# One ScalarE instruction writes the first f16 part of a tile to both of its places; VectorE copies only the second part

## The chip, the core and the metric

The kernel runs on one core of a Trainium2 chip. Its engines are TensorE (PE in the profile; PEld is its weight load), VectorE (DVE), ScalarE (ACT), GpSimd (POOL) and SyncE (SP). The metric is the device time of one execution in microseconds, as the median of several runs; lower is better.

## The reference

Eight sequences of 256 tokens with 512 features go through two layers. Layer 0 is a causal self-attention whose keys and values are both a context tensor (16 heads of 32), followed by a mixture of 32 experts (top 8). Layer 1 is a cross-attention with projected and RMS-normalised queries and keys, an output projection, and a ternary linear layer. Cut to what matters here:

```python
x = x + tanh(g_xattn[0]) * causal_attention(layernorm(x), ctx, ctx)          # layer 0: scores = q k^T per head
x = x + tanh(g_ffn[0])   * top8_of_32_experts(layernorm(x), gate_w, w_gate, w_up, w_down)
q = rms_norm(layernorm(x) @ w_q.T + b_q, g_q); k = rms_norm(ctx @ w_k_img.T + b_k_img, g_k_img)
x = x + tanh(g_xattn[1]) * (softmax(q k^T * s) v @ w_o.T + b_o)              # layer 1
x = x + tanh(g_ffn[1])   * (layernorm(x) @ ternary(weight).T + bias)
```

## The kernel before, in words

The program has three stages, one after the other: layer 0's attention, the experts, layer 1's attention.

**The f16 parts.** TensorE works on f16 operands, but f32 accuracy is wanted. So a f32 tile is split into a first part `hi = f16(x * scale)` and a second part `lo = f16(x * scale - hi)`. For the scores each head of 32 features gets four slots of 32 in the tile `parts[:, j, head, 0:4, :]`, so that the 128 rows of one matmul sum all products of parts. A query tile (`j < QT`, that is j = 0, 1) has the order hi, hi, lo, lo; a key tile (j = 2, 3) has hi, lo, hi, lo. `act_hi` on ScalarE writes the hi part to slot 0 (L349), `dve_lo` on VectorE computes the lo part (L355), waits for it, and then duplicates both parts into the two slots that are left with one copy of 1024 elements (L361). TensorE then transposes the finished tile in 16 small transposes (`pe_stack`, L372), and VectorE or ScalarE copies the result out of PSUM (`dve_stack`, L379, or `act_stack`, L318) to where the score matmuls read it.

**The attention loop.** Both layers run a loop of 8 batches (sequences) by 16 steps; each step is two heads of one query tile. A step has the score matmuls (L240, with a mask matmul L243 in layer 0), the row maximum on VectorE (L325) and its bias (L327), the exponential on ScalarE (L293), a transpose on TensorE (L278), a copy of it on ScalarE (L305), and the product with the values (L258). Tables written by hand (`PREP0`, `POST0`, `PREP1`, `POST1`) put the side work of the next batch (prep) and of the batch before (post) into given steps of each engine. Every engine runs its instructions in program order and meets the others by semaphores. In layer 0 the hi parts of the two context tiles are the piece "c" in step 3 on ScalarE (behind the piece "y0", L681, of the post work) and step 4 on VectorE; those of the two query tiles are the piece "q" in step 6, behind "S1" (L318). In layer 1 the four tiles are the pieces k0 to k3, one at a time, in steps 7, 8, 10 and 11 on ScalarE. Each layer splits 4 tiles for each of 8 batches, 64 tiles in all; the first 4 of each layer are split ahead of its loop.

**The experts.** 160 blocks of 128 tokens pass through a software pipeline. In step t TensorE transposes the input of block t+1 (L1293), multiplies block t by the gate and up weights (`gate_up`, L1305, 12 matmuls), transposes the hidden tile of block t-2 (L1316) and multiplies block t-3 by the down weights (L1329). `gate_up(t)` waits for the weights and for `h_ready` of block t-2, which VectorE's last instruction on that block sets (L1420). When a new expert begins, VectorE also splits its weights, in an early part at the end of one step (L1433 and L1436) and a late part at the start of the next (L1436). At the start of each step TensorE and VectorE load a number from a table in SBUF (`t_pe`, L1335, and `t_dve`, L1449) that says which expert comes and what to split. SyncE does the same with its own table (`t_x`, L1157), and its load already has bounds in the source (`min_val`, `max_val`).

Of the kernel before, what the change touches and what calls it, by code (L numbers as in the profile page):

```python
# [15 lines left out]
ACT = mybir.ActivationFunctionType  # L16
# [5 lines left out]
QT = S // P  # L22
HC = H // P
NH, D = 16, 32
# [65 lines left out]
def rep(ap, n, at):  # L90

    dims = [list(d) for d in ap.ap]
    dims.insert(at, [0, n])
    return bass.AP(ap.tensor, ap.offset, dims)
# [96 lines left out]
class Attention:  # L191
# [154 lines left out]

    def act_hi(self, act, b, i, src, scale):
        act.wait_ge(self.stack_ps, 8 * b.n + 2 * i + 2)
        self.nc.scalar.activation(self.part(ORDER[i], 0), src.rearrange("p (h d) -> p h d", d=D), ACT.Copy, scale=scale)\  # L349
          .then_inc(self.hi_ready, 1)  # L350

    def dve_lo(self, dve, b, i, src, scale, chain):
        j = ORDER[i]
        dve.wait_ge(self.hi_ready, 4 * b.n + i + 1)
        chain.link(self.nc.vector.scalar_tensor_tensor(self.part(j, 1), src.rearrange("p (h d) -> p h d", d=D), scale,  # L355
                                                       self.part(j, 0), ALU.mult, ALU.subtract))
        if j < QT:
            dup, of = self.parts[:, j, :, 1:4:2, :], self.parts[:, j, :, 0:4:2, :]
        else:
            dup, of = self.parts[:, j, :, 2:4, :], self.parts[:, j, :, 0:2, :]  # L360
        self.nc.vector.tensor_copy(dup, of).then_inc(self.parts_ready, 1)  # L361

    def pe_stack(self, pe, b, k):

# [746 lines left out]
def experts(nc, shared, plan, proj, w_experts, mats, ternary, ctx, vecs):  # L1111

    es = ExitStack()
    with es:
# [166 lines left out]
        @block.tensor  # L1281
        def _(pe):
            id32, id16 = shared.id32, shared.id16

            pe.sem_inc(y_ps, 1)

            def turn(t):
                pe.wait_ge(x_in[t.place], 16 * t.oct + 16)
                if t.at(-2).exists():
                    pe.wait_ge(x_ready, t.n - 1)  # L1290
                rows, o = xg[:, t.place, 0:H].bitcast(F16), bX[t.place % 2][:, :].bitcast(F16)
                for c in range(2 * HC):
                    last = nc.tensor.transpose(o[:, c * P : (c + 1) * P], rows[:, c * P : (c + 1) * P], id16[:])  # L1293
                last.then_inc(x_ps, 1)

            def gate_up(t, e):
                w = e & (NW - 1)
                pe.wait_ge(x_ready, t.n + 1)
                pe.wait_ge(weights_ready, e + 1)
                if t.at(-2).exists():  # L1300
                    pe.wait_ge(h_ready, t.n - 1)
                passes = [(0, wh), (0, wl), (H, wh)]
                for c in range(HC):
                    for k, (xo, wp) in enumerate(passes):
                        last = nc.tensor.matmul(bGU[t.place % 2][:, 0:GU], xT[:, t.place % 2, xo + c * P : xo + (c + 1) * P],  # L1305
                                                wp[:, bass.ds(w, 1), c * GU : (c + 1) * GU].rearrange("p a w -> p (a w)"),
                                                start=c == 0 and k == 0, stop=c == HC - 1 and k == 2)
                last.then_inc(gu_ps, 1)

            def turn_h(t):  # L1310
                pe.wait_ge(h_ready, t.n + 1)
                if t.at(-2).exists():
                    pe.wait_ge(ht_ready, t.n - 1)
                o = bHT[t.place % 2][:, :].bitcast(F16)
                for c in range(3):
                    last = nc.tensor.transpose(o[:, c * P : (c + 1) * P], hp[:, t.place % 2, c * P : (c + 1) * P], id16[:])  # L1316
                last.then_inc(ht_ps, 1)

            def down(t, e):
                w = e & (NW - 1)  # L1320
                pe.wait_ge(ht_ready, t.n + 1)
                if t.at(-2).exists():
                    pe.wait_ge(y_ready, t.n - 1)
                hi, lo, rest = (hT[:, t.place % 2, c * P : (c + 1) * P] for c in range(3))
                full, part = HC * GU, HC * GU + H
                products = [(hi, wh, full), (hi, wl, full), (lo, wh, full), (rest, wh, part),
                            (rest, wl, part)]
                for k, (h, wp, at) in enumerate(products):
                    last = nc.tensor.matmul(bY[t.place % 2][:, :], h,  # L1329
                                            wp[:, bass.ds(w, 1), at : at + H].rearrange("p a w -> p (a w)"),  # L1330
                                            start=k == 0, stop=k == len(products) - 1)
                last.then_inc(y_ps, 1)

            def step(t):
                code = pe.value_load(t_pe[0:1, t.column()])  # L1335
                e, before = code & (E - 1), code >> 5
                if t.at(1).exists():
                    turn(t.at(1))
                gate_up(t, e)
                if t.at(-2).exists():  # L1340
                    turn_h(t.at(-2))
                if t.at(-3).exists():
                    down(t.at(-3), before)
            turn(Tile(0, 0, 0))
            over_tiles(pe, step)
            last = Tile(MT - 1, (MT - 1) % 8, (MT - 1) // 8)
            turn_h(last.at(-1))
            turn_h(last)
            for t in (last.at(-2), last.at(-1), last):
                down(t, pe.value_load(t_e[0:1, t.column()]))  # L1350
# [51 lines left out]
        @block.vector  # L1402
        def _(dve):
            v = nc.vector

            def hidden(t):
                dve.wait_ge(silu, t.n + 1)
                if t.exists() and t.at(-1).exists():
                    dve.wait_ge(h_ready, t.n)
                v.scalar_tensor_tensor(hv[:, :], bGU[t.place % 2][:, FI:GU], SC_H / (SC_N * SC_W), sg[:, t.place % 2, :],  # L1410
                                       ALU.mult, ALU.mult).then_inc(h_made, 1)
                dve.wait_ge(h_made, t.n + 1)
                if t.at(-2).exists():
                    dve.wait_ge(ht_ps, t.n - 1)
                p, rest = hp[:, t.place % 2, :], FI - P
                v.tensor_copy(p[:, 0:P], hv[:, 0:P]).then_inc(h_hi, 1)
                v.tensor_copy(p[:, 2 * P : 2 * P + rest], hv[:, P:FI]).then_inc(h_hi, 1)
                dve.wait_ge(h_hi, 2 * t.n + 2)
                v.tensor_tensor(p[:, P : 2 * P], hv[:, 0:P], p[:, 0:P], ALU.subtract)
                v.tensor_tensor(p[:, 2 * P + rest :], hv[:, P:FI], p[:, 2 * P : 2 * P + rest], ALU.subtract).then_inc(h_ready, 1)  # L1420


            LATE = 3 * WEXP // 10

            def split(e, freed, early, late):

                w = e & (NW - 1)
                pick = lambda m, a, b: m[:, bass.ds(e & (NR - 1) if m is raw else w, 1), a:b].rearrange("p a w -> p (a w)")
                if early:
                    if freed is not None:  # L1430
                        dve.wait_ge(y_ps, freed + 1)
                    dve.wait_ge(raw_ready, e + 1)
                    v.tensor_scalar(pick(wh, 0, WEXP), pick(raw, 0, WEXP), SC_W, None, ALU.mult).then_inc(w_hi, 1)  # L1433
                dve.wait_ge(w_hi, e + 1)
                for a, b in ((0, LATE),) * early + ((LATE, WEXP),) * late:
                    last = v.scalar_tensor_tensor(pick(wl, a, b), pick(raw, a, b), SC_W, pick(wh, a, b), ALU.mult, ALU.subtract)  # L1436
                if late:
                    last.then_inc(weights_ready, 1)

            for t in range(3):  # L1440
                e = dve.value_load(t_e[0:1, t : t + 1])
                if t == 0:
                    split(e, None, True, True)
                else:
                    with dve.If(dve.value_load(t_new[0:1, t : t + 1]) > 0):
                        split(e, None, True, t == 1)

            def step(t):
                code = dve.value_load(t_dve[0:1, t.column()])  # L1449
                with dve.If((code & 1) > 0):  # L1450
                    split((code >> 2) & (E - 1), None, False, True)
                hidden(t)
                with dve.If((code & 2) > 0):
                    split((code >> 7) & (E - 1), code >> 12, True, False)

            over_tiles(dve, step, turn=4)


# [503 lines left out]
```

## Time and profile before

| | |
|---|---|
| median of 3 runs | 1558.1 us (1552.81, 1558.10, 1558.12) |
| span of the profiled execution, first to last instruction | 1525.3 us |
| median less span | 32.8 us |
| layer 0's attention | about 0 to 265 us of the span |
| experts | about 345 to 960 us |
| layer 1's attention | about 1012 to 1525 us |
| busy share of the span: PE, DVE, ACT, POOL | 86%, 64%, 60%, 34% |

The profiled execution has no time of its own outside the trace, so its span stands beside the median of the runs: the span leaves out what lies before the first and behind the last instruction of the program. A busy share is a mean over three stages with different limits. In the rows further down, a timeline row has its start and its length in us, the engine, the line, the operation, output<-input and the count, and in square brackets how long the engine was idle ahead of it and which instruction ended that.

### The profile page before, as it was taken

How to read it: one execution, taken by the hardware profiler on the slowest of the kernel's cores; microseconds unless marked ns; L12 is line 12 of the kernel's file. 1: busy time of each engine (PE TensorE's matmuls, PEld its weight loads, DVE VectorE, ACT ScalarE, POOL GpSimd, SP SyncE). 2: the span in 40 equal slices, each digit the busy share in tenths (PEclk: the TensorE clock that was granted, in tenths of full speed). 3: DMA queues.
4: the chain of work that ended last, by engine and by line, in shares of the span. 5: the costliest groups of instructions: out<-in, count | busy, mean ns of one | idle time of the engine just before them, and what ended most of it. 6: DMA issues, size and time to landing. Idle time of an engine off the chain costs nothing.

```text
span 1525.3 us, 37150 instructions
## 1 busy us (share of the span) xinstructions
PE 1309.4 (86%) x10733; PEld 834.6 (55%) x10734; DVE 972.8 (64%) x2387; ACT 920.1 (60%) x2261; POOL 520.1 (34%) x531
## 2 busy tenths in 40 slices
PE   5888888837999999999999999477989889898984
PEld 3656655524556666665666666144556555555552
DVE  5888888755456665655655633255787777776853
ACT  4777777724556666666666666244766667667661
POOL 1044444455333433332000001665554444541000
PEclk9988888968999999999999999688999999999997
DMA  2044344458888767767676545775654555642000
GB/s 72 29 173 180 146 146 151 156 213 304 269 285 282 256 219 261 238 217 244 218 242 222 181 149 154 126 111 83 98 99 65 104 82 84 100 65 52 15 1 28
DMA packets 96131, 233.39 MB, mean 153 GB/s; under 512 B 11808, under 2 KB 11808, under 8 KB 91424
## 3 DMA queue, kind: packets, MB, share of 16 engines
q0 software_dynamic: 33712, 113.79, 29.8%
q1 hardware_dynamic: 62320, 118.34, 23.3%
q8 instruction: 55, 0.90, 0.3%
q14 instruction: 44, 0.36, 0.1%
HBM read 140.84 MB, written 91.24 MB: 152 GB/s over the span
## 4 chain that ended last, share of the span: by engine, by line
PE 45%; DMA 9%; DVE 9%; issue 8%; ACT 3%; POOL 3%; SPq 1%; DVEq 0%; ACTq 0%; POOLq 0%
PE bank L1305 18%; PE bank L1329 10%; PE bank L1542 6%; DMA xs<-y_tiles,slot_ix 5%; PE bank L1293 4%; PE bank L258 2%; PE bank L1316 1%; PE bank L278 1%; DMA xg<-x_slots 1%; DVE l_nmax L325 1%; PE bank L1548 1%; POOL xs L430 1%; DMA x_slots<-blank 1%; DVE l_stack L379 1%; PE bank L240 1%
## 5 line engine op out<-in xcount | busy, mean ns | idle before, releaser
L1305 PE MATMUL bank<-wh,xT 128*128 x1280 | 343.3, 330 | 4.7 <-DVE hp L1420 4.4
L430 POOL DMA_INDIRECT xs<-y_tiles,slot_ix x120 | 194.6, 1622 | 234.2 <-DMA y_tiles<-ysb 99.1
L293 ACT ACTIVATE l_probs<-bank,l_bias 128x256 f32<-128x256 f32 (+1 forms) x512 | 224.4, 449 | 64.4 <-DVE l_bias L327 64.0
L1305 PE MATMUL bank<-wl,xT 128*128 x640 | 211.4, 330 | 0.0
L325 DVE TENSOR_REDUCE l_nmax<-bank 128x2 f32<-128x512 f32 (+1 forms) x256 | 158.1, 617 | 70.8 <-PE bank L240 41.3
L1410 DVE SCALAR_TENSOR_TENSOR hv<-bank,sg 128x192 f32<-128x192 f32 x160 | 56.9, 356 | 227.5 <-ACT sg L1364 203.5
L1379 ACT ACTIVATE ysb<-bank,xg 128x512 f32<-128x512 f32 x160 | 109.9, 687 | 119.1 <-PE bank L1329 119.1
L305 ACT ACTIVATE l_probsT<-bank 128x512 f32<-128x512 f32 (+1 forms) x256 | 140.0, 547 | 65.6 <-PE bank L278 65.2
L1358 ACT ACTIVATE xT<-bank 128x1024 f16<-128x1024 f16 x160 | 162.5, 1016 | 15.0 <-PE bank L1293 14.8
L1305 PEld LDWEIGHTS bank<-wh,xT 128*128 128x128 f16 x1280 | 126.5, 99 | 81.3 <-issue 11.1
L1329 PE MATMUL bank<-wh,hT 128*128 x480 | 156.1, 380 | 0.9 <-issue 0.9
L240 PE MATMUL bank<-l_stack 128*128 128x256 f16 (+1 forms) x512 | 105.7, 275 | 59.1 <-ACT l_probs L293 49.3
L278 PE MATMUL bank<-id,l_probs 128*128 128x128 f32 x896 | 149.7, 286 | 2.1 <-ACT l_probsT L305 0.5
L699 POOL DMA_INDIRECT x_slots<-room,slot_ix x112 | 113.4, 1013 | 108.3 <-issue 47.0
L1542 PE MATMUL bank<-w_hi,halfT 128*128 128x512 f16 x384 | 125.9, 390 | 18.9 <-DVE accb L1659 17.1
L1200 POOL DMA_DIRECT2D raw<-in_experts_dram x30 | 16.8, 560 | 334.1 <-DVE wl L1436 333.8
L1364 ACT ACTIVATE sg<-bank 128x192 f32<-128x192 f32 x160 | 52.8, 330 | 113.8 <-PE bank L1305 113.8
L1329 PE MATMUL bank<-wl,hT 128*128 x320 | 121.4, 379 | 0.0
L1293 PEld LDWEIGHTS bank<-id,xg 128*128 128x128 f16 x1280 | 84.9, 99 | 58.7 <-DMA xg<-x_slots 22.6
L1293 PE MATMUL bank<-id,xg 128*128 128x128 f16 x1280 | 98.9, 221 | 19.1 <-DMA xg<-x_slots 18.9
L278 PEld LDWEIGHTS bank<-id,l_probs 128*128 128x128 f32 x896 | 102.6, 147 | 11.7 <-ACT l_probsT L305 7.4
L1436 DVE SCALAR_TENSOR_TENSOR wl<-raw,wh x64 | 95.4, 1491 | 20.0 <-issue 15.9
(246 smaller groups left out, 2538.1 us busy)
## 6 DMA issues: line engine op xcount, KB each, us to landing
xg<-x_slots SPq DMA_DIRECT2D x160, 272.0 KB, 2.8
y_tiles<-ysb SPq DMA_DIRECT2D x160, 256.0 KB, 2.5
raw<-in_experts_dram POOLq DMA_DIRECT2D x30, 1280.0 KB, 7.1
x_slots<-blank SPq DMA_DIRECT2D x33, 272.0 KB, 3.6
xs<-in_x_dram SPq DMA_DIRECT2D x8, 512.0 KB, 4.4
cbuf<-in_ctx_dram SPq DMA_DIRECT2D x8, 512.0 KB, 5.8
stage<-in_mats_dram POOLq DMA_DIRECT2D x4, 1024.0 KB, 7.8
room<-in_ctx_dram SPq DMA_DIRECT2D x8, 512.0 KB, 4.6
```

Of the source, the lines that this page charges most:

```text
L240: last = self.nc.tensor.matmul(o, self.stack[:, b.par, 0, h, qt * P : (qt + 1) * P], self.stack[:, b.par, 1, h, 0:nk], start=True, stop=no ...
L278: last = self.nc.tensor.transpose(self.pT[s % len(self.pT)][:, (2 * kt + u) * P : (2 * kt + u + 1) * P], self.probs[:, s % 2, u, kt * P : ...
L293: last = self.nc.scalar.activation(self.probs[:, s % 2, u, 0:nk], self.pS[s % 2][:, u * S : u * S + nk], ACT.Exp, bias=self.bias[:, s % 4, ...
L305: self.nc.scalar.activation(self.probsT[:, s % 2, 0:w], self.pT[s % len(self.pT)][:, 0:w], ACT.Copy).then_inc(self.probsT_made, 1)
L325: self.nc.vector.tensor_reduce(self.nmax[:, s % 4, :], v, AX, ALU.max).then_inc(self.max_made, 1)
L430: return nc.gpsimd.indirect_dma_start(to, None, self.y_tiles[0 : (MT + 1 - k) * P, :], ix, compute_op=ALU.add)
L699: nc.gpsimd.indirect_dma_start(shared.x_slots, bass.IndirectOffsetOnAxis(ap=slot_ix[:, QT * b.n + t, k % TOPK : k % TOPK + 1], axis=0), xe ...
L1293: last = nc.tensor.transpose(o[:, c * P : (c + 1) * P], rows[:, c * P : (c + 1) * P], id16[:])
L1305: last = nc.tensor.matmul(bGU[t.place % 2][:, 0:GU], xT[:, t.place % 2, xo + c * P : xo + (c + 1) * P], wp[:, bass.ds(w, 1), c * GU : (c + ...
L1329: last = nc.tensor.matmul(bY[t.place % 2][:, :], h, wp[:, bass.ds(w, 1), at : at + H].rearrange("p a w -> p (a w)"), start=k == 0, stop=k ...
L1358: nc.scalar.activation(xT[:, t.place % 2, :], bX[t.place % 2][:, :].bitcast(F16), ACT.Copy).then_inc(x_ready, 1)
L1542: last = nc.tensor.matmul(o, xT[:, xo + c * P : xo + (c + 1) * P], w[:, c * H : (c + 1) * H], start=n == 0, stop=n == len(todo) - 1)
```

## The change

Three edits.

```diff
     def act_hi(self, act, b, i, src, scale):
         act.wait_ge(self.stack_ps, 8 * b.n + 2 * i + 2)
-        self.nc.scalar.activation(self.part(ORDER[i], 0), src.rearrange("p (h d) -> p h d", d=D), ACT.Copy, scale=scale)\
+        j = ORDER[i]
+        twice = self.parts[:, j, :, 0:2, :] if j < QT else self.parts[:, j, :, 0:3:2, :]
+        self.nc.scalar.activation(twice, rep(src.rearrange("p (h d) -> p h d", d=D), 2, 2), ACT.Copy, scale=scale)\
           .then_inc(self.hi_ready, 1)

     def dve_lo(self, dve, b, i, src, scale, chain):
...
-        if j < QT:
-            dup, of = self.parts[:, j, :, 1:4:2, :], self.parts[:, j, :, 0:4:2, :]
-        else:
-            dup, of = self.parts[:, j, :, 2:4, :], self.parts[:, j, :, 0:2, :]
-        self.nc.vector.tensor_copy(dup, of).then_inc(self.parts_ready, 1)
+        self.nc.vector.tensor_copy(self.parts[:, j, :, 3, :], self.part(j, 1)).then_inc(self.parts_ready, 1)
```

The source of the ScalarE instruction is read twice (a repeated dimension of stride 0), 1024 elements instead of 512, and goes to both hi slots. The copy on VectorE moves 512 elements instead of 1024. No instruction is added or taken away here, and the waits are the same.

```diff
             def step(t):
-                code = pe.value_load(t_pe[0:1, t.column()])
+                code = pe.value_load(t_pe[0:1, t.column()], min_val=0, max_val=E * E)
...
             for t in range(3):
-                e = dve.value_load(t_e[0:1, t : t + 1])
+                e = dve.value_load(t_e[0:1, t : t + 1], min_val=0, max_val=E - 1)
...
             def step(t):
-                code = dve.value_load(t_dve[0:1, t.column()])
+                code = dve.value_load(t_dve[0:1, t.column()], min_val=0, max_val=2**24)
```

These give three table loads of the experts' stage bounds, and a load with bounds is followed by instructions that test them. They stand in the program as two more instructions behind each load (shown as ISA x2). On VectorE, at the late part of a weight split, a step begins like this before (`raw` is an expert's loaded weights, `wl` their second f16 part, ISA a register instruction):

```order
L1453 UNCONDITIONAL_BRANCH
L1449 ISA
L1449 TENSOR_LOAD t_dve
L1450 REGISTER_ALU
L1450 COMPARE_AND_BRANCH
L1434 REGISTER_ALU x3
L1436 REGISTER_ALU
L1436 ISA
L1436 REGISTER_ALU
L1436 ISA
L1436 SCALAR_TENSOR_TENSOR wl<-raw,wh 128x1792
```

and like this in the changed program, whose line numbers are two lower there:

```order
L1451 UNCONDITIONAL_BRANCH
L1447 ISA
L1447 TENSOR_LOAD t_dve
L1447 ISA x2
L1448 REGISTER_ALU
L1448 COMPARE_AND_BRANCH
L1432 REGISTER_ALU x3
L1434 REGISTER_ALU
L1434 ISA
L1434 REGISTER_ALU
L1434 ISA
L1434 SCALAR_TENSOR_TENSOR wl<-raw,wh 128x1792
```

Nothing else moved; the two instructions stand between the load and the branch that leads to the split. On TensorE a step of the experts begins like this before (`xg` is a loaded block, `xT` its transpose, `wh` the first part of the weights):

```order
L1335 TENSOR_LOAD t_pe
L1293 MATMUL bank<-id,xg 128x128 x8
L1299 REGISTER_ALU x2
L1305 REGISTER_ALU
L1305 ISA
L1305 MATMUL bank<-wh,xT 128x384
```

and in the changed program:

```order
L1333 TENSOR_LOAD t_pe
L1333 ISA x2
L1291 MATMUL bank<-id,xg 128x128 x8
L1297 REGISTER_ALU x2
L1303 REGISTER_ALU
L1303 ISA
L1303 MATMUL bank<-wh,xT 128x384
```

The two instructions stand ahead of the transposes of the next block.

## Rows read from the trace of the kernel before

**Rows 1.** The page: busy time of each engine, share of the span, instructions.

```profile
PE 1309.4 (86%) x10733; PEld 834.6 (55%) x10734; DVE 972.8 (64%) x2387; ACT 920.1 (60%) x2261; POOL 520.1 (34%) x531
```

**Rows 2.** Stretches of layer 0, experts, layer 1: us; busy per engine; granted clock.

```profile
20.00:265.00 245.00, 197.72 (x1997) 145.45 (x1996) 204.36 (x567) 177.17 (x614) 92.80 (x93) 0.88 0.35 128
460.00:960.00 500.00, 496.43 (x3779) 308.40 (x3776) 275.69 (x753) 312.69 (x543) 106.64 (x127) 1.00 0.67 222
1012.00:1480.00 468.00, 415.93 (x3532) 259.69 (x3532) 337.54 (x671) 304.60 (x831) 190.57 (x159) 0.98 0.45 74
```

**Rows 3.** Groups by form, ACT: busy, mean ns of one, idle before.

```profile
L349 ACT ACTIVATE l_parts<-cbuf 128x512 f16<-128x512 f32 x16 | 9.1, 615 | 3.0 <-DMA cbuf<-in_ctx_dram 3.0
L305 ACT ACTIVATE l_probsT<-bank 128x512 f32<-128x512 f32 x192 | 115.1, 600 | 64.3 <-PE bank L278 64.0
L305 ACT ACTIVATE l_probsT<-bank 128x256 f32<-128x256 f32 x64 | 24.9, 389 | 1.2 <-PE bank L278 1.2
```

**Rows 4.** Groups by form, DVE.

```profile
L361 DVE COPY l_parts<-l_parts 128x1024 f16<-128x1024 f16 x64 | 27.4, 428 | 2.2
L355 DVE SCALAR_TENSOR_TENSOR l_parts<-cbuf,l_parts 128x512 f16<-128x512 f32 x16 | 11.0, 688 | 0.0
L750 DVE COPY cum<-cum 128x32 f16<-128x32 f16 x8 | 1.3, 167 | 0.0
```

**Rows 5.** Timeline, layer 0: PE in batches 0, 1, 4, 4.

```profile
33.66 0.62 PE L372 MATMUL bank<-id,l_parts 128*128 128x128 f16 x8 [1.20 <-DVE l_parts L361]
...
65.99 0.29 PE L240 MATMUL bank<-l_stack 128*128 128x128 f16 x1 [1.22 <-ACT l_probs L293]
...
178.02 0.29 PE L240 MATMUL bank<-l_stack 128*128 128x128 f16 x1 [1.22 <-ACT l_probs L293]
...
184.47 0.61 PE L372 MATMUL bank<-id,l_parts 128*128 128x128 f16 x8 [0.31 <-ACT l_stack L318]
```

**Rows 6.** Timeline, layer 0, batch 4: ACT and DVE around the two pairs.

```profile
176.14 1.13 ACT L349 ACTIVATE l_parts<-cbuf 128x512 f16<-128x512 f32 x2
...
184.22 1.14 ACT L349 ACTIVATE l_parts<-room 128x512 f16<-128x512 f32 x2
...
184.88 0.69 DVE L355 SCALAR_TENSOR_TENSOR l_parts<-room,l_parts 128x512 f16<-128x512 f32 x1
...
187.01 0.68 DVE L325 TENSOR_REDUCE l_nmax<-bank 128x2 f32<-128x512 f32 x1
```

**Rows 7.** Timeline, layer 1, the batch prepared from 1228 us: ACT, DVE, PE.

```profile
1231.92 0.60 ACT L305 ACTIVATE l_probsT<-bank 128x512 f32<-128x512 f32 x1 [1.31 <-PE bank L278]
...
1244.85 0.63 ACT L349 ACTIVATE l_parts<-accb 128x512 f16<-128x512 f32 x1 [1.96 <-DVE accb L1666]
...
1245.52 0.69 DVE L355 SCALAR_TENSOR_TENSOR l_parts<-accb,l_parts 128x512 f16<-128x512 f32 x1
...
1246.44 0.39 PE L240 MATMUL bank<-l_stack 128*128 128x256 f16 x2 [0.27 <-ACT l_probs L293]
...
1254.42 0.61 PE L1548 MATMUL bank<-id,a 128*128 128x128 f16 x8 [1.39 <-DVE a L1731]
```

**Rows 8.** One line's instructions: SyncE's load with bounds, VectorE's without (ns min/median/max).

```profile
L1157 SPq FUSED_REGOPS  x280: 46/152/162, 342.1 to 939.2; - x140
L1157 SPq SEQ_ASSERT  x160: 18/18/18, 342.3 to 939.4; - x160
...
L1449 DVEq TENSOR_LOAD <-t_dve x160: 300/307/1347, 347.4 to 952.0; - x160
```

**Rows 9.** Timeline, experts: DVE and PE at the first, the last of eleven places.

```profile
465.56 0.24 DVE L1420 TENSOR_TENSOR hp<-hv,hp 128x64 f16<-128x64 f32 x1
466.14 0.33 PE L1305 MATMUL bank<-wh,xT 128*128 x1
...
729.19 2.03 DVE L1436 SCALAR_TENSOR_TENSOR wl<-raw,wh  x1 [0.68 <-issue]
...
762.37 0.33 PE L1305 MATMUL bank<-wh,xT 128*128 x1
```

## The prediction

> **What bounds the kernel now.** I read the page first: TensorE is busy 86% of the span, VectorE 64%, ScalarE 60% [rows 1]. That mean hides three stages, so I read the stretches next [rows 2]. In the experts TensorE is busy 496.4 of 500 us at the full clock, so only what makes TensorE wait can cost there. In layer 0 no engine is full: TensorE 198, VectorE 204 and ScalarE 177 of 245 us, and the granted clock is 0.88, so part of it runs at the lower level, 1.2 instead of 2.4 GHz. That is a loop in which the three engines wait for each other in turn, and a longer instruction counts exactly where its engine is the one waited for. Layer 1 is in between (TensorE 416 of 468). So I took the timeline around each of the split tiles and asked each time who waits for whom.
>
> **Prices.** *ScalarE.* The edit makes each of 64 instructions twice as long in elements. The copies of 512 and of 256 elements take 600 and 389 ns [rows 3]: 0.82 ns an element, so 512 more cost (600 - 389) / 256 x 512 = 0.42 us, and 0.615 us becomes 1.04. Upper bound: a second whole instruction, which the pairs show to start 0.52 us behind the first (1.13 us for two of 0.615, [rows 3, 6]). No row lets 512 more elements pass for less than 0.42; I keep 0.30 as the lower end. Total 64 x 0.42 = 27 us of ScalarE.
>
> *VectorE.* The copy has 512 f16 elements for 1024. 32 elements take 167 ns and 1024 take 428 [rows 4]; on that line 512 take 0.29, so each copy saves 0.135 us, 8.6 us in all. The new copy has the same runs of 32 elements as the old one. Bounds: it can't take less than 0.167; at worst it goes at the pace of the other 512-element instruction, 0.688, and costs 0.26 more than now. I take 0.29, since its nearest row is the old copy.
>
> *The bounds tests.* They have nothing to do with the rest of the change. VectorE and TensorE don't show one, but SyncE does: behind its load stand a register instruction of 152 ns and an assert of 18 ns, 0.17 us together [rows 8]. These durations leave out what lies between two instructions; I take 0.25 us for each load, 0.17 as the lower end and 0.5 as the upper. The Trainium skill (Perfetto Trace Analysis, section Per-engine timelines) says that for a sequencer instruction the profiler reports only its execution and not fetch, decode and push. By the bare 0.17 the experts' 3.5 us below would be 2.1.
>
> **Layer 0.** Take batch 4. The pair "c" starts at 176.14 directly behind L681, the exponentials follow it without a gap, and TensorE has been idle 1.22 us when it gets them at 178.02 [rows 5, 6]. ScalarE is what is waited for, so both added stretches are passed on: 2 x 0.42 = 0.85 us. Then TensorE has no gap until 184.47 [rows 5], so it carries the 0.85 along; VectorE's two shorter copies buy nothing, because its next piece waits for TensorE's transposes. At 184.47 it waits for L318 on ScalarE, itself behind TensorE, so still 0.85. Now the pair "q" at 184.22. VectorE's L355 at 184.88 starts the moment the first hi part is there, so it starts 0.42 later; then L355, copy, L355, copy run to the maximum at 187.01 [rows 6], where two copies give back 0.27. Net 0.15 at the maximum. ScalarE is later by the whole 0.85, but TensorE is then busy in the gate's matmuls and sees about 0.18 of it. I take 0.17 for "q". Per batch 0.85 + 0.17 = 1.02 us. The wait of 1.22 us stands in six batches, from 65.99 on [rows 5] (the others up to 253.05): 6 x 1.02 = 6.1. In batch 0, where no post work stands ahead, TensorE waits for VectorE's copy instead (1.20 us at 33.66 [rows 5]), and the shorter copies give about 0.3 back; the last batch splits nothing. Layer 0: 5.8 us.
>
> Two things can move this. The lower clock level returns to the upper one around 183 in this batch, so work pushed behind it runs faster and gives some of the 0.85 back; or more idle time makes the low stretch longer. I price neither and give layer 0 the range 3 to 9.
>
> **Layer 1.** k0 and k1 are hidden: k0 has its exponentials ready just as TensorE ends a projection, and at 1231.92 ScalarE has waited 1.31 us for TensorE [rows 7]; k1 stands ahead of another projection. Cover there is thin for k0 (0.4 us): gone, it costs up to 0.4 us a batch. k2 at 1244.85 ends a wait of 1.96 us for VectorE, and its hi part starts L355 at 1245.52: 0.42 later. TensorE, which waits for the exponentials at 1246.44, is 0.42 later there too. But that isn't what is late next: from 1245.52 VectorE works without a gap up to the L1731 that TensorE waits 1.39 us for at 1254.42 [rows 7]. Both copies, k2's and k3's, stand in that run. k3's longer ScalarE instruction is hidden beside it, with 0.35 us to spare. So 0.42 - 2 x 0.135 = 0.15 us a batch, 7 batches: 1.1 us. The four tiles split ahead of the loop add 0.3 at most; taken 0.3.
>
> **Experts.** `gate_up` starts at the earliest 0.34 us behind L1420 of two blocks before (465.80 to 466.14 [rows 9]). In eleven blocks between 460 and 770 us the distance is exactly that, the last at 762.37 [rows 9], so VectorE is waited for; in eight more it is 0.1 to 0.2 longer. All nineteen follow a split of new weights, where the late part starts 0.68 us late because of VectorE's own sequencer [rows 9]: load (0.307 [rows 8]), branch, addresses. The test stands right there, exposed: 11 x 0.25 + 5 x 0.12 + 3 x 0.05 = 3.5 us. In the other blocks L1420 is done earlier than that, so their tests are free. On TensorE the sequencer runs ahead of the engine by more than 0.25 us in nearly every block; I allow 0.5 us for those right after a stall. Experts: 4.0 us, between 1 and 8.
>
> **Sum.** 5.8 + 1.1 + 0.3 + 4.0 = 11.2 us on the profiled execution's span of 1525.3: 1536.5. The median of the runs lies 32.8 us above that span, so 1558.1 + 11.2 = 1569.3 us, 0.7% slower. I say 1569. A measurement of this kernel can tell about 0.5% (7.8 us) from no change: the three runs of before already spread by 5.3 us.
>
> **Rivals.**
> *All is passed on* (chance 0.18). Nothing hides "q", k2 and k3: layer 0 6 x 4 x 0.42 = 10, layer 1 7 x 0.7 = 5, experts 4 to 8: 1576 to 1581. For it: the waits for ScalarE's exponentials are in both layers. Against it: the gapless runs on VectorE behind "q" and k2.
> *The copy falls out of its fast pace* (0.05): 0.688 instead of 0.29. Where VectorE is waited for (two copies in six batches of layer 0 and in seven of layer 1) that is 26 x 0.4 = 10 us more: 1580.
> *The loop swallows it* (0.22): the later start of "c" falls into slack I don't see, or is given back by the clock, and the tests hide behind the load: layer 0 3, layer 1 0, experts 1: 1562. It is inside 0.5%.
> *Shorter copies win* (0.05). VectorE is the busiest engine of layer 0. If every one of the 64 copies counted and no ScalarE instruction and no test did, the gain would be 8.6 us: 1549.5. The point from which it decides: the 512 added elements must cost ScalarE's successors less than the 0.27 of two copies. The wait of 1.22 us for ScalarE in six batches speaks against it. The Trainium skill (Perfetto Trace Analysis, Optimizing Scalar/DVE Operations) speaks against it too: an operation with a fast mode on VectorE is quicker there, and moving work to ScalarE may pay only when VectorE is saturated. The rows say 0.135 against 0.42 us, and 83% in the fullest stage. By that rule the change loses 0.285 us on each tile, 18 us if all 64 counted: 1576, the edge of the first rival, whose chance it shares.
> *Forecast* 0.50: 1564 to 1575.
>
> **How the numbers follow.** Low end: layer 0 3, layer 1 and prologue 0, experts 1 give 1562; high end: layer 0 9, layer 1 5, experts 8 give 1580. 1561 to 1580 leaves out most of the faster case, some of the smallest and some of the two large ones, 2 in 10. Slower by over 0.5% takes most of the forecast's 0.50 and the two large cases: 0.70. Within 0.5%: the swallowed case and the forecast's lower edge, 0.26. Faster: 0.04.
>
> **What the profile of after would show.** L349's successor at about 1.04 us (1.14 with the pointer scale), the copy at 0.29. In layer 0 the wait for the exponentials at 1.22 grown to about 2.1 in six batches, and a batch about 1.0 us longer. In layer 1 a batch longer by 0.15, the wait of 0.27 grown to 0.7, that of 1.39 nearly unchanged. In the experts a SEQ_ASSERT behind each load, the gap of 0.68 grown to 0.93, the waits of `gate_up` for L1420 grown by 3.5 us in all. The prediction is wrong if the wait at 1.22 grows and the batch doesn't, if the clock's low stretches change in number, or if the tests cost TensorE's sequencer so much that TensorE has gaps in ordinary blocks: 0.1 us in each of 160 would be 16 us.

## The result, and the profile after

| | before | after |
|---|---|---|
| median of 7 runs each | 1556.69 us (1552.81 to 1558.12) | 1565.13 us (1558.26 to 1568.90) |
| ratio, 95% interval | | 1.0046 (1.0023 to 1.0068), +7.2 us |
| profiled execution: time, span | (span 1525.3) | 1558.26, 1556.5 |

Slower, by just under the 0.5% that the prediction took as what can be told from no change. The +7.2 us are the ratio's; the two medians lie 8.4 us apart. 1569 us was forecast, between 1561 and 1580. The forecast's own step was +11.2 us.

The page's busy times of the changed kernel, for [rows 1]:

```profile
PE 1313.1 (84%) x10733; PEld 836.0 (54%) x10734; DVE 964.9 (62%) x2387; ACT 949.1 (61%) x2261; POOL 517.1 (33%) x531
```

and its stretches of layer 0, experts and layer 1, for [rows 2] (length, busy time of PE, PEld, DVE, ACT and POOL, granted clock, DMA share, GB/s):

```profile
20.00:291.00 271.00, 200.49 (x2019) 147.25 (x2016) 203.93 (x580) 192.18 (x620) 91.44 (x93) 0.87 0.32 116
493.00:985.00 492.00, 485.94 (x3687) 301.70 (x3686) 272.51 (x740) 304.95 (x528) 100.36 (x120) 1.00 0.67 220
1045.00:1512.00 467.00, 416.03 (x3538) 259.45 (x3539) 334.41 (x672) 317.79 (x835) 190.22 (x158) 0.98 0.46 74
```

ScalarE has 29 us more work (27 forecast), VectorE 8 less (8.6 forecast). But the stretch of layer 0 that took 245 us now takes 271, far more than the whole change in time. Two facts undo the puzzle. A time is its execution's span plus 1.8 us (1558.26 and 1556.5), so the profile of before, with a span of 1525.3, was not taken in an execution like the timed 1553 to 1558 us, and the 32.8 us between them are not "around" the span. And the runs below fell on four chips, of two kinds: on one kind the kernel before takes 1521 to 1523 us, on the other 1556 to 1558. By the length of its batches in layer 0 the profile of before is of the first kind, that of after of the second. (Each chip was used once, so that the chip itself makes the difference is inferred; no run shows it.) So the changed kernel was profiled again on a chip of the first kind (run e2_after_again, span 1534.8), and its rows can be laid beside those of before.

Its groups by form, for [rows 3, 4]:

```profile
L359 DVE COPY l_parts<-l_parts 128x512 f16<-128x512 f16 x64 | 19.0, 296 | 2.2
L351 ACT ACTIVATE l_parts<-accb,rs 128x1024 f16<-128x1024 f32 x16 | 18.2, 1141 | 0.1
...
L351 ACT ACTIVATE l_parts<-cbuf 128x1024 f16<-128x1024 f32 x16 | 15.9, 1042 | 3.2 <-DMA cbuf<-in_ctx_dram 3.2
```

1.04 us and 0.30 us for 1.04 and 0.29 forecast. Layer 0, batch 3, for [rows 5, 6]:

```profile
140.91 1.99 ACT L351 ACTIVATE l_parts<-cbuf 128x1024 f16<-128x1024 f32 x2
...
143.65 0.29 PE L240 MATMUL bank<-l_stack 128*128 128x128 f16 x1 [2.07 <-ACT l_probs L293]
...
149.84 1.99 ACT L351 ACTIVATE l_parts<-room 128x1024 f16<-128x1024 f32 x2
...
150.09 0.61 PE L370 MATMUL bank<-id,l_parts 128*128 128x128 f16 x8 [0.31 <-ACT l_stack L318]
...
150.92 0.69 DVE L357 SCALAR_TENSOR_TENSOR l_parts<-room,l_parts 128x512 f16<-128x512 f32 x1 [0.41 <-ACT l_parts L351]
...
152.80 0.68 DVE L325 TENSOR_REDUCE l_nmax<-bank 128x2 f32<-128x512 f32 x1
```

TensorE's wait of 1.22 us is 2.07, in six batches (on both kinds of chip). Behind the pair "q" the maximum stands 2.96 us after the pair's start (152.80 - 149.84), 2.79 before: +0.17, as worked out. Layer 1, the batch of [rows 7]:

```profile
1254.61 0.69 DVE L357 SCALAR_TENSOR_TENSOR l_parts<-accb,l_parts 128x512 f16<-128x512 f32 x1 [0.46 <-ACT l_parts L351]
...
1255.54 0.39 PE L240 MATMUL bank<-l_stack 128*128 128x256 f16 x2 [0.67 <-ACT l_probs L293]
...
1263.19 0.61 PE L1546 MATMUL bank<-id,a 128*128 128x128 f16 x8 [0.88 <-DVE a L1729]
```

0.27 became 0.67 (0.7 forecast). The other wait was to stay at about 1.39 and is 0.88. Experts, for [rows 8] (the register instructions of a line, with ns min/median/max):

```profile
L1447 DVEq FUSED_REGOPS  x274: 46/190/192, 356.5 to 961.4; - x137
L1447 DVEq TENSOR_LOAD <-t_dve x160: 300/307/1360, 356.1 to 961.0; - x160
L1447 DVEq SEQ_ASSERT  x160: 23/23/33, 356.7 to 961.6; - x160
...
L1333 PEldq TENSOR_LOAD <-t_pe x160: 296/516/1300, 353.9 to 958.1; - x160
```

and from the timeline, for [rows 9], a late part of a split:

```profile
736.59 2.03 DVE L1434 SCALAR_TENSOR_TENSOR wl<-raw,wh  x1 [0.94 <-issue]
```

The test is there, and the gap of 0.68 us is 0.94 (0.93 forecast).

### The profile page after: what moved, and what is told of

It reads as the page before. It is cut to its first block, busy times and chain, and to the rows that moved or that the text cites. A ratio compares the mean times of both kernels' runs of the same rounds, so it can differ in the third digit from the quotient of the medians.

```text
span 1556.5 us, 37796 instructions
## 1 busy us (share of the span) xinstructions
PE 1313.1 (84%) x10733; PEld 836.0 (54%) x10734; DVE 964.9 (62%) x2387; ACT 949.1 (61%) x2261; POOL 517.1 (33%) x531
## 4 chain that ended last, share of the span: by engine, by line
PE 43%; issue 8%; DMA 8%; DVE 8%; ACT 4%; POOL 2%; SPq 1%; DVEq 1%; POOLq 0%; ACTq 0%
PE bank L1303 18%; PE bank L1327 9%; PE bank L1540 5%; DMA xs<-y_tiles,slot_ix 5%; PE bank L1291 4%; PE bank L258 2%; DMA xg<-x_slots 2%; PE bank L278 1%; PE bank L1314 1%; POOL xs L428 1%; DVE l_nmax L325 1%; PE bank L1546 1%; ACT l_probs L293 1%; PE bank L240 1%; DVE l_stack L377 1%
## 5 line engine op out<-in xcount | busy, mean ns | idle before, releaser
L293 ACT ACTIVATE l_probs<-bank,l_bias 128x256 f32<-128x256 f32 (+1 forms) x512 | 225.0, 450 | 58.9 <-DVE l_bias L327 58.5
L240 PEld LDWEIGHTS bank<-l_stack 128*128 128x128 f16 x512 | 45.8, 101 | 125.4 <-ACT l_probs L293 80.4
```

The source lines that it names most:

```text
L240: last = self.nc.tensor.matmul(o, self.stack[:, b.par, 0, h, qt * P : (qt + 1) * P], self.stack[:, b.par, 1, h, 0:nk], start=True, stop=no ...
L293: last = self.nc.scalar.activation(self.probs[:, s % 2, u, 0:nk], self.pS[s % 2][:, u * S : u * S + nk], ACT.Exp, bias=self.bias[:, s % 4, ...
```

## The experiments

Twelve kernels ran, on four chips, each beside the kernel before on its own chip. A batch of layer 0 is given without the f16 edit there, as the mean of batches 2 to 6 of a trace (e3, e5, e12, e13). The kernel before was not profiled again, so its rows are those of one execution.

| chip of | before, median | one batch of layer 0 |
|---|---|---|
| e2, e3, e4 | 1522.98 us | 37.5 us |
| e5 to e8 | 1555.95 us | 42.5 us |
| e9 to e12 | 1521.26 us | 37.5 us |
| e13 | 1557.66 us | 41.7 us |

**e2_after_again** is the changed kernel, unchanged. Theory A takes the profiled execution of before for an unusual one; theory B says that a profiled execution leaves some 33 us out.

> The changed kernel, unchanged, once more, on the same chip as its parts. Ratio 1.0046 expected (1.002 to 1.007), +7 us. Theory A: span about 1.8 us below its time and layer 0 batches of 40.5 to 43 us. Theory B: the same span, but far from that of before.

1536.60 us against 1522.98, ratio 1.0086 (1.0068 to 1.0104), +13.6 us between the medians. Span 1534.8. By the ratios the same change costs 13 us on this chip and 7 on the first; the two intervals just meet. Neither theory had it fully: the profile of before was of an ordinary execution, of another kind of chip.

**e3_tests_only.** The three loads bounded, `act_hi` and `dve_lo` as before.

```diff
-                code = pe.value_load(t_pe[0:1, t.column()])
+                code = pe.value_load(t_pe[0:1, t.column()], min_val=0, max_val=E * E)
...
-                code = dve.value_load(t_dve[0:1, t.column()])
+                code = dve.value_load(t_dve[0:1, t.column()], min_val=0, max_val=2**24)
```

> Only the bounds tests of the three table loads; the f16 parts are written as before. Theory 1 (as forecast): the test stands exposed at the late part of a weight split, +4.0 us (1 to 8), the distance of 0.68 us ahead of the late part grows to 0.93. Theory 2 (the tests hide, since the experts' stage of the changed kernel is 605.25 us long against 605.2): 0 us, ratio 1.000, and the whole 7 us comes from the f16 parts. Theory 3 (the tests are everything): +7 us.

1529.85 us, ratio 1.0048 (1.0028 to 1.0068), +6.9 us: nearly twice the 4.0. So the tests are half of the change on this chip, not a small part, and theory 2 is gone.

**e4_cost_alone.** The changed kernel with the old copy.

```diff
-        self.nc.vector.tensor_copy(self.parts[:, j, :, 3, :], self.part(j, 1)).then_inc(self.parts_ready, 1)
+        if j < QT:
+            dup, of = self.parts[:, j, :, 1:4:2, :], self.parts[:, j, :, 0:4:2, :]
+        else:
+            dup, of = self.parts[:, j, :, 2:4, :], self.parts[:, j, :, 0:2, :]
+        self.nc.vector.tensor_copy(dup, of).then_inc(self.parts_ready, 1)
```

> The changed kernel with VectorE's copy of 1024 elements put back: ScalarE's longer instruction without VectorE's gain. By my terms the shorter copies give back 6 x 0.27 in layer 0, 7 x 0.27 in layer 1 and 0.3 + 0.3 in the prologues: 4.1 us, so this kernel is 4 us slower than the changed one (+11 us against before where the changed one is at +7). Rival (VectorE's copies buy nothing, because its next piece waits for TensorE anyway): the same time as the changed kernel. Rival (the copy counts everywhere): +8.6 us against the changed kernel.

1539.02 us, ratio 1.0112 (1.0085 to 1.0139): 2.4 us behind the changed kernel by the medians and 4.0 by the ratios, where 4 was expected. The intervals of the two overlap, so the times decide little. The traces say more. In layer 0 a batch takes 38.70 us here and 38.76 in e2, so there the shorter copies give back nothing that can be seen. In layer 1 a steady batch takes 61.37 us against 61.08: 0.29, which is the two copies' 0.27.

**e5_mask_only** takes the place of the kernel before as a base without tests: the value that a wait uses is masked, so that it can't be negative.

```diff
-                e = dve.value_load(t_e[0:1, t : t + 1])
+                e = dve.value_load(t_e[0:1, t : t + 1]) & (E - 1)
...
-                    split((code >> 7) & (E - 1), code >> 12, True, False)
+                    split((code >> 7) & (E - 1), (code >> 12) & 255, True, False)
```

> The f16 parts as before, no bounds test anywhere; instead the freed block's number is masked with 255 in the early split (one register operation per weight split, none on the other loads), and the three prologue loads with 31. It is the base for the parts of the edit without the tests. Theory 1 (the tests' price is the instructions behind each of the 320 loads): ratio 1.000, within 0.1% of before, gaps ahead of the late split at 0.68 us as before. Rival (any register work on VectorE's sequencer between load and split costs): +2 us or more.

1557.29 us, ratio 1.0017 (0.9999 to 1.0035). By the interval the base itself costs between nothing and 5 us; the next kernels are read against it. Its trace shows that the mask is not free. The early part of a split follows the masked number on VectorE's sequencer, and the idle time ahead of it grew by 0.12 us each (12.0 us of "issue" over 26, then 15.7 over 27, between 460 and 960 us; before, then e5_mask_only):

```profile
L1433 DVE TENSOR_SCALAR wh<-raw x26 | 38.8, 1494 | 13.0 <-issue 12.0 <-POOLq L1207 1.0
```

```profile
L1433 DVE TENSOR_SCALAR wh<-raw x27 | 40.4, 1495 | 17.6 <-issue 15.7 <-POOLq L1207 1.4 <-PE bank L1329 0.6
```

The blocks that wait for a late part are 0.12 us longer too (4.45 to 4.57, 4.43 to 4.55, 3.82 to 3.94). So the rival has a part of it.

**e6_hi_mask** is the whole edit of the f16 parts on that base, **e7_hi_layer0** and **e8_hi_layer1** one layer of it (a condition `self.causal` on the new lines of `act_hi` and `dve_lo`, and its opposite).

> The whole edit of the f16 parts, with the mask in place of the tests. Theory 1 (the parts add up): the last chip gave +13.6 us for the changed kernel and +6.9 for the tests alone, so +6.7 us here; layer 0's batches 38.2 to 39.1 us against 37.4. Forecast by my own terms: 5.8 + 1.1 + 0.3 = 7.2. Rival (tests and parts hide each other, only one counts): +10 us or more or under +3.

1555.72 us, ratio 1.0003 (0.9988 to 1.0017): nothing, or 1.6 us less than the base. On the other kind of chip the same edit costs about 13.6 - 6.9 = 6.7 us.

> The edit of the f16 parts in layer 0 alone, with the mask. Forecast by my terms: 5.8 us (1.02 us in each of six batches, -0.3 in the first). By the traces of the changed kernel (batches +0.8 to +1.7 us): +7 us at the end of layer 0, of which the experts' start may give some back. Rival (layer 1 carries the cost): under +2 us.

1560.00 us, ratio 1.0027 (1.0010 to 1.0043), 2.7 us above the base, with intervals that overlap: less than the 5.8, perhaps nothing.

> The edit of the f16 parts in layer 1 alone, with the mask. Forecast by my terms: +1.1 us, up to +0.3 more in its prologue. Rival (the copies win there, since VectorE ends last in most batches; the trace of the changed kernel has layer 1's eight batches 0.3 us shorter than before): -0.5 to 0 us.

1553.10 us, ratio 0.9991 (0.9976 to 1.0006), 4.2 us below the base, whose interval it meets only at the edge. The sign of the layer 1 term was wrong. The two layers add up to the whole: 2.7 - 4.2 = -1.5 us, against e6's -1.6.

**e9_hi_c** and **e10_hi_not_c** divide it once more, on the other kind of chip: `self.causal and j >= QT` takes the pair "c" alone, `not self.causal or j < QT` all the rest (query tiles of layer 0, and layer 1).

> The edit of the f16 parts for the two context tiles of layer 0 alone (the pair c), with the mask in place of the tests. My term: 2 x 0.42 = 0.85 us passed on in each of six batches, 5.1 us, less 0.3 in the first batch. On a chip whose layer 0 has batches of 37.4 us before: +4.8 us. On one where they are 42.3 us before, the last two chips say that something else sets the pace and takes up part of it: 0 to +3 us. Rival (the context tiles are free and the query tiles carry the cost): 0 us, and the next kernel is slower by 5.

1530.39 us, ratio 1.0065 (1.0039 to 1.0090), +9.1 us, nearly twice the 4.8. The trace doesn't bear out so much: its first seven batches of layer 0 take 258.3 us in sum against 253.7 before, 4.6 more. The mask is in the 9.1 too; what else is in it is not located.

> The edit of the f16 parts everywhere but for those two tiles: query tiles of layer 0 and all of layer 1, with the mask. Forecast by my terms: 6 x 0.17 + 1.1 + 0.3 = +2.4 us. By the traces since: steps 7 and 8 of a batch of layer 0 together 0.3 us shorter or 0.16 longer by the place of the low clock, layer 1 shorter by 0.3 to 4 us, so -1 to -4 us, which would make this the quickest form, ratio 0.998 to 0.9995.

1523.79 us, ratio 1.0017 (0.9999 to 1.0035), the same as the base had against before on the other kind of chip, so the rest of the edit costs nothing that can be told. e9, with the same mask on the same chip, is 6.6 us slower: nearly all of the f16 edit's cost on this kind of chip is the pair "c". My +2.4 fits the +2.5 as it stands. The later -1 to -4 fits only if the mask costs a few us here as well, and the mask alone wasn't run on this kind.

**e11_tests_dve** and **e12_tests_again**: the tests on VectorE's loads alone (`t_pe` without bounds), and all three once more.

> The bounds tests on VectorE's loads alone (TensorE's load of its table has none), f16 parts as before. Theory 1 (VectorE's late split is what is exposed; TensorE's sequencer runs ahead): all but 0.5 us of the cost of the tests, so about +6.4 us where both cost 6.9. Rival (TensorE's own test is half of it, since the trace shows new idle time ahead of the transposes of the next block): +3 us.

1525.25 us, ratio 1.0023 (1.0007 to 1.0039), +4.0 us.

> All three bounds tests, f16 parts as before, once more beside the kernel with VectorE's alone, on the same chip: +6.9 us (1.003 to 1.007) whatever the chip, since in the experts' stage the blocks of all traces are 3.64 us long and only the blocks with a change of weights differ. Rival (the cost depends on the chip as that of the f16 parts does): under +3 us on a chip with the longer layer 0.

1529.84 us, ratio 1.0061 (1.0035 to 1.0086), +8.6 us. So TensorE's test is half of it, 4.6 us between the medians, for which 0.5 was forecast; the rival had it. (The two intervals still touch; by their single runs it lies between 1 and 7 us.) That the cost is the same on the other kind of chip was not run alone; there the changed kernel (+7.2) and the f16 parts (0) leave about 7 us for the tests.

**e13_merged.** No tests, the f16 edit in layer 1 alone, the mask, and the two parts of a weight split issued together.

```diff
-                        split(e, None, True, t == 1)
+                        split(e, None, True, True)
...
-                with dve.If((code & 1) > 0):
-                    split((code >> 2) & (E - 1), None, False, True)
                 hidden(t)
                 with dve.If((code & 2) > 0):
-                    split((code >> 7) & (E - 1), code >> 12, True, False)
+                    split((code >> 7) & (E - 1), (code >> 12) & 255, True, True)
```

> No tests, the edit of the f16 parts in layer 1 alone, the mask, and one more edit: the two parts of a weight split, which stand next to each other on VectorE with only a table load and a branch between them, are issued together at the end of a step. In the traces VectorE is idle 0.68 us ahead of each of 26 late parts (0.9 with the tests), and the blocks right behind are the ones that are longer than 3.64 us. Theory 1 (that stretch of VectorE's sequencer is what the experts wait for): the idle time there falls to 0.1 us, the longer blocks between 460 and 770 us shrink by about 0.3 to 0.5 us each in some 14 places, 4 to 7 us less, plus the 1 to 4 us that layer 1 gave: ratio 0.993 to 0.998. Rival (the load and the branch then stand exposed ahead of the next block's work on the hidden tile instead): 0.998 to 1.000.

1546.77 us against 1557.66, ratio 0.9925 (0.9896 to 0.9955), 10.9 us faster than before, at the better end of the theory's 0.993 to 0.998, and well ahead of e8 (0.9991, on another chip). The expectation misread one thing: in the trace of before the 26 late parts between 460 and 960 us wait 13.1 us in all, only eight of them 0.68 us each, most of the others 0.29 or 0.40. Groups of the experts between 460 and 960 us of e12_tests_again, and then of e13_merged, whose lines are eight higher:

```profile
L1305 PE MATMUL bank<-wh,xT 128*128 x1063 | 281.1, 326 | 3.3 <-DVE hp L1420 2.9 <-issue 0.2
...
L1293 PE MATMUL bank<-id,xg 128*128 128x128 f16 x1048 | 79.9, 219 | 3.3 <-issue 1.7 <-DMA xg<-x_slots 1.2
...
L1436 DVE SCALAR_TENSOR_TENSOR wl<-raw,wh x50 | 74.6, 1492 | 20.8 <-issue 17.6
```

```profile
L1313 PE MATMUL bank<-wh,xT 128*128 x1083 | 287.1, 327 | 0.1
...
L1444 DVE SCALAR_TENSOR_TENSOR wl<-raw,wh x54 | 78.1, 1488 | 3.5
```

With the load and the branch gone from between the two parts, VectorE's 17.6 us of "issue" ahead of them are gone and `gate_up` waits 0.1 us for anything. From the first `gate_up` to the last e13's trace takes 593.3 us, e8's 599.0. Its layer 0 is 4.5 us shorter as well, which the edit doesn't touch. So of the 10.9 us the joined parts account for some 6 by the trace, and layer 1 for up to 4.

## Why the prediction was right or wrong

**The experts (4.0 us forecast, 6.9 and 8.6 measured).** This term was mis-sized. I read the distance from one `gate_up` to the next in each trace; an ordinary block takes 3.64 us in all of them. What blocks 40 to 157 take above that, in sum:

| kernel | excess over 3.64 us | blocks over 3.70 us |
|---|---|---|
| before | 5.3 us | 13 |
| e11, VectorE's tests | 7.3 us | 17 |
| e3, e12, all tests | 10.6, 11.4 us | 26, 26 |
| changed kernel, first chip and e2; e4 | 9.7, 10.3; 10.6 us | 26, 23; 28 |
| e5 to e10, no tests, the mask | 5.2 to 6.9 us | 12 to 18 |
| e13, parts together | 0.9 us | 4 |

The first 40 blocks are left out: there TensorE waits mostly for loaded blocks (`xg`, 18.9 us in the trace of before), their excess lies between 14 and 21 us, and it doesn't follow the edits. For that reason the whole stage doesn't show the tests so cleanly (603.4 us from the first `gate_up` to the last before, 605.4 in e12, 610.1 in e3). The table shows where the tests cost; how much they cost in all is the medians' to say.

VectorE's share went as described: at eight of the eleven places blocks are 0.26 to 0.30 us longer in e11 (4.45 to 4.74, 4.43 to 4.70, 3.82 to 4.10), 0.25 forecast. In sum it is 1.9 us here, under the 3.5 forecast, while e11's median is 4.0 us above before. The step that failed is "On TensorE the sequencer runs ahead of the engine by more than 0.25 us in nearly every block; I allow 0.5 us". The reserve holds on average, but not where it is smallest. TensorE's load of its table takes 0.31 us at best but up to 1.4. These rows are that line in e11_tests_dve, without its test, and in e12_tests_again, with it:

```profile
L1335 PEldq TENSOR_LOAD <-t_pe x160: 297/308/1174, 345.8 to 950.6; - x160
```

```profile
L1335 PEldq TENSOR_LOAD <-t_pe x160: 297/547/1377, 345.2 to 950.9; - x160
L1335 PEldq SEQ_ASSERT  x160: 18/18/24, 346.4 to 951.7; - x160
```

And from the timeline of e12_tests_again a place where nothing waited before:

```profile
836.66 0.61 PE L1293 MATMUL bank<-id,xg 128*128 128x128 f16 x8 [0.35 <-issue]
```

At 836.66 the load had taken 1.35 us, and load and test together were more than the sequencer had in hand; that block is 4.35 us long, 3.64 before. With TensorE's test nine more blocks are above 3.70 us, and the sum is 3.4 to 4.1 us larger, near the 4.6 of the medians. That the median load itself rises from 0.31 to 0.55 us was not foreseen; why it does stays open.

**Layer 0 (5.8 us forecast).** The mean of the steps between exponentials (ACT L293, 16 steps a batch, mean of batches 2 to 6) says where a batch grows:

| | batch | steps 0 to 2 | step 4 | steps 7 to 9 | step 12 | steps 14, 15 |
|---|---|---|---|---|---|---|
| before, quicker kind | 37.47 | 4.42 | 5.11 | 9.41 | 2.29 | 2.86 |
| e9, "c" alone, quicker kind | 38.20 | 4.42 | 5.96 | 9.29 | 2.29 | 2.86 |
| e10, "q" alone in layer 0, quicker kind | 37.50 | 4.41 | 5.11 | 9.32 | 2.39 | 2.87 |
| e2, both, quicker kind | 38.76 | 4.41 | 5.96 | 9.63 | 2.47 | 2.88 |
| e5, neither, slower kind | 42.48 | 5.63 | 5.11 | 10.13 | 2.56 | 5.65 |
| e6, both, slower kind | 42.40 | 5.48 | 5.96 | 9.50 | 2.48 | 5.60 |

Step 4 takes the forecast's 0.85 us to the hundredth, in every kernel that has the edit on "c", on both kinds of chip. "q" alone costs 0.03 us a batch here, 0.17 forecast (steps 7 to 9 are 0.09 shorter, step 12 is 0.10 longer). Both together are 1.29 us, 1.02 forecast, and more than the sum of the parts. The step "work pushed behind it runs faster and gives some of the 0.85 back; or more idle time makes the low stretch longer" was left unpriced, and both happen. Between 20 and 265 us the granted clock of e10_hi_not_c is higher than before's 0.88 [rows 2]:

```profile
20.00:265.00 245.00, 190.81 (x2004) 140.87 (x2004) 204.50 (x571) 182.99 (x614) 93.88 (x93) 0.91 0.35 128
```

while in e2, where the low stretches no longer come once a batch at one place, single batches are 0.5 us longer at step 7 or 12. So layer 0 costs about 7.8 us over its seven full batches in e2's trace, inside the range of 3 to 9.

On the other kind of chip the same 0.85 is there at step 4, and the batch is no longer. Steps 7 to 9 are 0.63 us shorter with the edit, since those of the base are 0.7 longer than on the first kind; 0.3 more comes out of the rest. That is the "loop swallows it" rival, true on these chips for the pair (0.4 us over seven batches between the traces of e5 and e7; the medians say 2.7, with 0 inside what they leave open). It is one reason why the first measurement fell below the forecast; the other is layer 1. The cause of 5 us more in each batch there is only located, not found. In the changed kernel's trace on the first chip:

```profile
127.29 0.61 PE L278 MATMUL bank<-id,l_probs 128*128 128x128 f32 x4
...
129.19 0.69 DVE L377 COPY l_stack<-bank 128x1024 f16<-128x1024 f16 x1 [2.25 <-remote]
130.00 0.10 PEld L240 LDWEIGHTS bank<-l_stack 128*128 128x128 f16 x1 [1.80 <-issue]
130.03 0.22 PE L240 MATMUL bank<-l_stack 128*128 128x128 f16 x1 [1.56 <-DVE l_stack L377]
...
130.74 0.60 ACT L305 ACTIVATE l_probsT<-bank 128x512 f32<-128x512 f32 x1 [2.73 <-remote]
```

VectorE and ScalarE both wait more than 2 us for TensorE's transposes, whose modelled ends are 126.5 and 127.9. It comes once a batch near step 14, in kernels with and without the edit. Whether TensorE itself is late there or only the news of its end, the profile does not show; I leave it open.

**Layer 1 (1.1 us forecast, -4.2 measured on the base in e8).** The chain on VectorE was read rightly: the wait at k2 is 0.67, and a steady batch takes 61.1 us against 60.9, near the forecast's 0.15. Wrong was "that of 1.39 nearly unchanged": it fell by 0.5. The forecast saw that k3's longer instruction is hidden behind VectorE's run, but not that TensorE, which waits for the exponentials behind k3, gets there later and so has less left to wait for L1731. The idle time moved some 3.6 us ahead; it didn't go. Before, then e2_after_again:

```profile
1250.28 0.39 PE L240 MATMUL bank<-l_stack 128*128 128x256 f16 x2 [1.13 <-ACT l_probs L293]
```

```profile
1259.60 0.39 PE L240 MATMUL bank<-l_stack 128*128 128x256 f16 x2 [1.35 <-ACT l_probs L293]
```

In a steady batch the two waits are 0.91 and 1.39 us before and 1.36 and 0.87 with the edit. What I had not counted is the clock. Six of seven traces without the edit in layer 1 have one to four stretches of 3.4 us at the lower level (1.2 GHz) in its second to seventh batch, each making a batch 0.5 to 2.5 us longer; none of the seven with it (e4 among them) has one. Most of these stretches begin about 59 us into the batch, one to two us behind the end of the wait of 1.39. Layer 1 of e11_tests_dve, one stretch in it and the whole, and then of e2:

```profile
1190.00:1200.00 10.00, 6.80 (x57) 4.64 (x58) 6.85 (x14) 7.55 (x22) 5.41 (x4) 0.84 0.68 133
...
1077.00:1444.00 367.00, 331.07 (x2813) 206.62 (x2809) 274.18 (x542) 242.63 (x648) 154.24 (x130) 0.98 0.46 74
```

```profile
1086.00:1449.00 363.00, 326.50 (x2822) 204.69 (x2823) 272.01 (x544) 253.60 (x651) 152.24 (x130) 1.00 0.46 76
```

The six batches take 361.9 to 367.5 us in the traces without the edit, 361.4 to 362.6 in those with all of it, and 363.9 in e4. That the edit in layer 1 ends the low stretches is shown by these counts, six of seven traces against none of seven. Why is not shown. It isn't VectorE's shorter copy, since e4 has the old one. It isn't less idle time of TensorE either: its waits of over 0.3 us sum to 5.5 us in a steady batch before, 6.1 in e2 and 6.3 in e4. The rows of e4_cost_alone in the same batch:

```profile
1262.76 0.39 PE L240 MATMUL bank<-l_stack 128*128 128x256 f16 x2 [1.36 <-ACT l_probs L293]
...
1266.47 0.61 PE L1550 MATMUL bank<-id,a 128*128 128x128 f16 x8 [1.00 <-DVE a L1733]
```

What fits all of them is that the wait just ahead of the place is shorter, 0.87 or 1.00 for 1.39, but no run changed that wait alone.

**The sum.** 5.8 + 1.1 + 0.3 + 4.0 = 11.2 was made on a profile of the quicker kind of chip. There the change costs 13.6 us: layer 0 some 8, the tests 7 to 9, less 1 to 4 in layer 1. On the kind that the median came from, layer 0 costs 2.7 us by e7 instead of 5.8 and layer 1 gives 4.2 by e8 instead of costing 1.4; together they come to about nothing (e6), and so the 7.2 are the tests, for which 4.0 was forecast. So no term was right there, and that the time fell inside the range is luck: the mistakes had both signs and nearly cancelled. Two of the prediction's own signs of being wrong came true, the wait at 1.22 that grows while the batch doesn't, and the low stretches of the clock that change in number. The sentence "The median of the runs lies 32.8 us above that span" should have stopped me: it was no frame around the span but another layer 0, 5 us longer in every batch.

## What to carry to other kernels

A difference of 2% between a profile's span and the timed median is not overhead until a profile with its own time has shown it: the loop may have another critical path in the executions that count, and slack that the trace does not show. A few register instructions behind a load are paid where the sequencer's lead over its engine is smallest, so look for the slowest load and the branch between two large instructions, not at the mean; taking such a load out from between two instructions that always follow each other was worth some 6 us here, more than anything the change gained. Copying to a second place in the longer engine's instruction costs its full length where that engine is waited for, 0.85 us a batch at the pair "c", unless the loop has slack further on. A steady batch of layer 1 became 0.2 us longer too; the 4 us gained there came with the clock, and that nobody can plan on until the cause is shown.

## What the runs showed of the hardware that was not expected

Chips differ by 2.2% on this kernel (1521 to 1523 us and 1556 to 1558), and all of it lies ahead of the experts, most in layer 0, 5 us a batch. About half of that stands in steps 14 and 15, where VectorE and ScalarE wait 2 to 3 us for TensorE's transposes. One table load on a sequencer takes from 0.30 to 1.54 us (the longest in e8), and TensorE's median goes from 0.31 to about 0.5 us (0.49 to 0.55) when a test follows it. A bounds test is 0.19 + 0.02 us of instructions on VectorE, 0.15 + 0.02 on TensorE, and moved VectorE's next engine instruction by 0.26. One masking operation moved it by 0.12. The Trainium skill (Perfetto Trace Analysis, section Per-engine timelines) says that what is reported of a sequencer instruction leaves out fetch, decode and push; with 0.26 against 0.21 the trace agrees.
